# Two transformer layers in one launch: the first attention's value products issued in pairs, its exponent ring lengthened from six units to eight

## The reference

```python
b, n, d = z.shape                                # 4, 1024, 128
qkv5 = (zn @ w_qkv).reshape(b, n, H, HD, 3)      # H = 16 heads of HD = 8
q, k, v = (jnp.transpose(qkv5[..., i], (0, 2, 1, 3)) for i in range(3))
scores = jnp.einsum('bhqd,bhkd->bhqk', q, k) / SCALING
att = jax.nn.softmax(scores, axis=-1)
out = jnp.einsum('bhal,bhlv->bhav', att, v)
out = jnp.transpose(out, (0, 2, 1, 3)).reshape(b, n, d)
return z + out @ w_proj + b_proj
```

## Time and profile before

| | |
|---|---|
| Time, three runs | 1762.59 us median (1762.27 to 1764.18) |
| The profiled execution: its own time | 1763.79 us |
| its span | 1762.1 us |
| PE busy in the span | 1411.1 us, 80% |
| DVE busy | 1127.6 us, 64% |
| ACT busy | 830.6 us, 47% |
| POOL busy | 193.1 us, 11% |
| Mean granted TensorE clock | 0.901 |
| First attention, from its first score unit to its last copy | 209.5 to 972 us |

### The profile page before, as it was taken

One profiled execution on the slowest core, in us unless ns is written; L12 is line 12 of the kernel. 1 busy time (PEld: TensorE's weight loads), 2 busy tenths in 40 slices (PEclk: granted clock), 3 DMA queues, 4 the chain that ended last, 5 costly groups with the idle time before them and its releaser, 6 DMA issues. The chain is left out here.

```text
span 1762.1 us, 29361 instructions
## 1 busy us (share of the span) xinstructions
PE 1411.1 (80%) x10529; PEld 681.9 (39%) x10529; DVE 1127.6 (64%) x1680; ACT 830.6 (47%) x988; POOL 193.1 (11%) x201
## 2 busy tenths in 40 slices
PE   3573999999999999999999288877996998788600
PEld 2441122222222222222221155545994555566500
DVE  4876988878878878888880366535554887111124
ACT  1330166666656666666668145433222555334200
POOL 2210000000000000000000000003771000000174
PEclk9775599999989999999999699989996999899855
DMA  3747111111111110111100211000110000323122
GB/s 79 252 159 208 55 53 41 41 42 41 41 40 41 38 44 6 41 41 40 41 7 8 63 36 36 12 12 2 41 48 28 17 15 5 91 83 108 33 64 71
DMA packets 77664, 93.52 MB, mean 53 GB/s; under 512 B 10836, under 2 KB 47532, under 8 KB 77012
## 3 DMA queue, kind: packets, MB, share of 16 engines
q1 hardware_dynamic: 73436, 83.38, 17.3%
q0 software_dynamic: 4096, 8.40, 1.6%
HBM read 46.24 MB, written 45.11 MB: 52 GB/s over the span
## 5 line engine op out<-in xcount | busy, mean ns | idle before, releaser
L527 DVE TENSOR_REDUCE b_mx<-psum 128x1 f32<-128x512 f32 x1024 | 644.4, 684 | 102.1 <-PE psum L604 100.0
L572 ACT ACTIVATE b_exp_ring<-psum 128x1024 f32<-128x1024 f32 x512 | 500.4, 1022 | 226.3 <-PE psum L635 225.7
L604 PE MATMUL psum<-b_k,b_q 96*128 96x512 bf16 x1024 | 376.5, 407 | 29.4 <-DVE b_v L516 26.6
L635 PE MATMUL psum<-b_q,b_k 96*128 96x512 bf16 x1024 | 310.2, 387 | 10.6 <-issue 9.3
L618 PE MATMUL psum<-b_exp_ring,b_v 128*32 128x512 f32 x2048 | 275.3, 610 | 17.7 <-ACT b_acc L564 17.4
L604 PEld LDWEIGHTS psum<-b_k,b_q 96*128 96x128 bf16 x1024 | 100.2, 99 | 366.8 <-DVE b_mx L527 248.4
L635 PEld LDWEIGHTS psum<-b_q,b_k 96*128 96x128 bf16 x1024 | 97.7, 99 | 120.0 <-ACT b_exp_ring L572 25.3
L1557 DVE TENSOR_TENSOR e_y<-psum,e_b 128x512 f32<-128x512 f32 (+1 forms) x24 | 13.3, 555 | 123.9 <-PE psum L1601 123.9
L923 POOL MEMSET c_credit<- 128x1 f32 x1 | 0.1, 103 | 826.3 <-POOLq L508 826.3
L618 PEld LDWEIGHTS psum<-b_exp_ring,b_v 128*32 128x32 f32 x2048 | 40.8, 108 | 122.9 <-issue 88.3
L1572 ACT ACTIVATE e_hT<-psum,e_b 128x358 f32<-128x358 f32 (+1 forms) x96 | 53.7, 559 | 68.5 <-PE psum L1591 64.8
(11 more groups left out here) (256 smaller groups left out, 1558.6 us busy)
## 6 DMA issues: line engine op xcount, KB each, us to landing
b_q<-q_ops SPq DMA_DIRECT2D x16, 600.0 KB
q_ops<-a_q SPq DMA_DIRECT2D x36, 256.0 KB, 3.5
k_ops<-a_k SPq DMA_DIRECT2D x36, 256.0 KB, 3.6
b_k<-k_ops SPq DMA_DIRECT2D x16, 576.0 KB
x_disp<-b_zeros SPq DMA_DIRECT2D x13, 320.0 KB
v_ops<-a_vs SPq DMA_DIRECT2D x4, 1024.0 KB, 5.6
b_v<-v_ops SPq DMA_DIRECT2D x16, 256.0 KB
av_out<-b_acc SPq DMA_DIRECT2D x128, 32.0 KB, 1.6
```

Of the source, the lines that this page charges most:

```text
L527: nc.vector.reduce_max(mx[:, block:block + 1], bank, AX.X)\
L572: act.activation(ex[:, n % E_RING, :, :], g.bank(b, 2).rearrange("p (h t) -> p h t", h=2), ACT.Exp, scale=ATT_SCALE).then_inc(sem("b_exp_d ...
L604: nc.tensor.matmul(g.bank(n % MAX_BANKS), q[s][:, h, t * P:(t + 1) * P], k[s][:, h, half * BANK:(half + 1) * BANK], start=True, stop=True)\
L635: last = nc.tensor.matmul(g.bank(4 + 2 * (u % 2) + i), k[s][:, h, kb * P:(kb + 1) * P], q[s][:, h, half * BANK:(half + 1) * BANK], start=T ...
```

## The change

The groups of value products are issued two at a time: groups 0 and 1 at unit 5, 2 and 3 at unit 9, and so on; the quad's last two at unit 1 of the next quad, or at the end of a loop turn. The first of a pair thus comes two units later than before, the second stays at its unit. The ring gets eight slots, and the credit becomes `AHEAD` = 4 groups. ScalarE's copies move one place, behind exponent 19, and 3 of the next quad. Instructions, sizes, the maxima's three banks and the order of everything else stay.

```diff
-E_RING = 6
+E_RING = 8
+AHEAD = E_RING // 2
...
-                act.wait_ge(sem("b_av"), val(j, GROUPS, 0, TB * (half + 1) + 3))
+                act.wait_ge(sem("b_av"), val(j, GROUPS, 0, TB * (half + 1) + AHEAD))
...
-                    if u == 2 and carry:
+                    if u == 3 and carry:
                         evacuate(j, 2 * c - 1)
-                    if u == 18:
+                    if u == 19:
                         evacuate(j, 2 * c)
...
                     if u == 1 and carry:
-                        times_v(j, c - 1, GROUPS - 1)
-                    if u >= 3 and u % 2:
-                        times_v(j, c, (u - 3) // 2)
+                        for group in (GROUPS - 2, GROUPS - 1):
+                            times_v(j, c - 1, group)
+                    if u >= 5 and u % 4 == 1:
+                        for group in ((u - 5) // 2, (u - 3) // 2):
+                            times_v(j, c, group)
                     for it in todo[1:]:
                         item(j, *it)
                 if flush:
-                    times_v(j, c, GROUPS - 1)
+                    for group in (GROUPS - 2, GROUPS - 1):
+                        times_v(j, c, group)
...
-            nc.gpsimd.memset(credit[:, 0:1], 0.0).then_inc(sem("b_av"), 3)
+            nc.gpsimd.memset(credit[:, 0:1], 0.0).then_inc(sem("b_av"), AHEAD)
...
-                    sp.wait_ge(sem("b_av"), val(j, GROUPS, c, GROUPS + 3))
+                    sp.wait_ge(sem("b_av"), val(j, GROUPS, c, GROUPS + AHEAD))
```

## The result

| | before | changed |
|---|---|---|
| Median of six runs | 1763.08 us (1762.27 to 1765.29) | 1775.45 us (1772.20 to 1780.77) |
| Ratio | | 1.0069, 95% interval 1.0051 to 1.0087 |
| Profiled execution: time, span | 1763.79, 1762.1 us | 1780.77, 1779.0 us |

The change made the kernel 0.7% slower, by 12.4 us between the medians and 17.0 us between the profiled executions.

What follows compares the result with a forecast made beforehand. TensorE was taken to bound the first attention stage, VectorE following closely. Intervals +19.6, quads' ends +9.1, copies -17.0 and tail +5.5 sum to +17.2: 1781.0 us profiled, 1780 forecast, range 1757 to 1803.

Steps and rivals of the forecast that it cites:

- The pair on TensorE: Value products on TensorE: a pair's second group takes 0.853 us, so a pair lasts 1.85 to the next maxima matmul.
- the saving of 0.24 us: TensorE time saved per pair of value-product groups; if nothing else moved, four units would take 5.42 us, not 5.66.
- The interval of 5.84: Steady four units: maxima matmuls wait for three banks, 5.84 us instead of 5.66, +0.18 in 109 intervals, +19.6.
- Quads' ends: Two intervals with extra VectorE work at each quad's end: 6.39 and 6.25 us, 14 quads x 0.65 = +9.1 us.
- The copy: Value products no longer wait 0.68 us for the accumulator's copy, 25 times: -17.0 us; two tail copies hidden: -2.4.
- The tail: Last quad after its maxima, ACT the bound: pairs 5.01 us apart instead of 4.17, +8.0, less 2.4 for copies, net +5.5.
- The rival that had it at the lower clock throughout: Tail at half clock: intervals of 7.4 us, +23 us, 1803 us in all; chance 0.07.
- The loop's edges: Around the loop's turns: the 3 to 5 us of idling stay, priced at nothing, 3 us allowed either way.
- The sum: Whole profiled execution: 19.6 + 9.1 - 17.0 + 5.5 = +17.2 us, from 1763.8 to 1781.0.
- The median: Median of runs: 1780 us, taking the profiled execution, 1781.0, as 1.2 over it.
- some 45 us: Sign to look for: TensorE idle before the maxima's matmuls, put to b_mx, some 45 us in all.

Runs made afterwards that it cites:

- the five-bank run: The changed kernel with five PSUM banks for the maxima instead of three, both heads of a score unit sharing one bank: 1732.14 us against 1764.76 for the kernel before, 0.9814.
- the run of the copy alone: The kernel before with only the accumulator's copies moved, behind exponents 17 and 1: 1743.94 us against 1764.53, 0.9883; in an earlier run 0.9892.
- second profile: The changed kernel run and profiled once more, nothing altered: 1855.13 us against 1842.91 for the kernel before, 1.0075.
- the ring: The kernel before with only the ring lengthened to eight units and credits of 4, value products still single: 1845.69 us against 1842.91, 1.0014.
- both with five banks: The changed kernel and the kernel before, each with five maxima banks and shared score banks: 0.9814 and 0.9980 against the kernel before.
- the short maxima: The changed kernel with three banks, each maximum over 256 of 512 columns and a smaller exponent scale: 1716.74 us against 1764.53 for the kernel before, 0.9735.

## Why the prediction was right

The mechanism was right and the sizes nearly so. By its own steps:

- **The pair on TensorE.** Second group at 0.853: measured 1.86 to the next M, against 1.00 for a lone group. Right, and so is the saving of 0.24 us: the five-bank run has 5.46 instead of 5.66, 0.04 of waiting included.
- **The interval of 5.84.** Measured 5.84 or 5.85, with each of the eight M within 0.01 us of where it was put. The cause is shown from three sides: more banks remove it, shorter maxima remove it, and another order of the M moves it to the predicted 6.17.
- **Quads' ends.** 6.39 and 6.25 forecast, 6.44 and 6.30 measured. But they cost more before, too, than the 0.31 that I took from one quad: over steady intervals 0.46 on average, by the distances of 2.86 and 3.22 named above. So 14 quads give +8.2 instead of +9.1.
- **The copy.** The wait is gone; -17.0 and -2.4 were forecast for all of them, and the run of the copy alone gives 20.6 (16.8 and 2.0 in the intervals concerned).
- **The tail.** Pairs at 5.01 forecast, 5.03 measured. The clock fell there after all, but for one pair: behind TensorE's wait of 1.31 us for the last quad's maximum of maxima, the pair at 935.91 took 3.20 us instead of 1.92. From the value products of unit 21 in the last quad but one to those of unit 29 in the last, the tail takes 54.03 us instead of 46.30: +7.7 where I had 5.5. In the second profile the same wait of 1.31 us is followed by a pair of 1.92, and the tail takes 52.40: +6.1. The rival that had it at the lower clock throughout is refuted.
- **The loop's edges.** Forecast to stay, within 3 us either way. In the profiles the eight intervals around the ends of turns are 3.8 us shorter in the changed kernel (63.24 instead of 67.07), and 6.2 shorter in its second profile. The clock is a large part of it: three turns at the lower level before, two and one in the changed kernel, at some 2.2 us each.
- **The sum.** +17.2 forecast for the profiled execution, +17.0 measured; so close an agreement is luck. In the stage itself the profiles differ by 14.9 us: +19.9 in the intervals (108 of them), +8.2 at quads' ends, -16.8 for the copies, +7.7 in the tail and -4.1 at the edges and in the first interval. The other 2.1 us lie before the stage (1.4) and behind it (0.8), where the change does nothing and I had forecast nothing.
- **The median** moved by less, +12.4. The term that was mis-sized is the edges' nothing. By an estimate from the profiles, the changed kernel has 1.4 turns at the lower clock where the kernel before has 3, which at 2.2 us each makes -3.5. I also took the profiled execution's distance from the median of before (1.2 us) for the changed kernel, and its own was 5.3. The 5.4 us between its two profiles, taken apart above, show what such a distance consists of.

What I said would show it and did not: "some 45 us" of TensorE idle before L605. The row has 20.5 put to `b_mx` (27.4 in all), for the reason given above: half of each stall hides in the displayed length of the matmul before it.

## What to carry to other kernels

Before two short jobs of one engine are joined into a long one, count how long the engine next to it can live on what is buffered: here three banks less the one being filled against 1.86 us without a matmul. The engine whose total is smaller (VectorE, 4.9 of 5.7 us) can still set the pace, and the joined version pays back the 0.24 us that it saves, and 0.18 more. And where a change hides a second, unrelated stall, look for the place where that stall costs nothing by itself: moving one copy by one unit gave 20 us with two numbers edited.

## What was not expected of the hardware

- The stage's steady intervals repeat to 0.01 us in every profile, while the whole kernel spreads by 8 us in six runs of one kind, and took 80 us more, in later stages, in one set of runs.
- Behind the hardware loop's turns the granted clock fell to its lower level in all 21 cases of the seven profiles in which TensorE hardly waits for a bank (the kernel before, the copy alone twice, the ring, both with five banks, the short maxima), and in 7 of 15 cases of the five profiles with pairs, three banks and whole maxima. Stalls of a few tenths of a us in each interval go with fewer such falls; why is not shown.
- After a wait of 1.31 us on TensorE in the last quad but one, one pair ran at the lower clock (3.20 us instead of 1.92) and the next at the full one. The same wait is in all five profiles of the changed kernel's kind; three of them have such a fall and two have not, so the wait alone does not bring it.
- Reading the same PSUM bank twice in one exponent, with two score matmuls written over each other, took the same time as two banks: interval 5.84 us in either.
